# Value experts of a two-layer transformer kernel: the expert as inner index of the columns

## The chip, the cores and the metric

The kernel runs on 1 core of one Trainium2 chip. The metric is the device time of one execution in microseconds (us). One program computes the whole network, four sequences one after the other in each layer.

## The reference, cut to what matters

The network takes 4 sequences of 1024 tokens of width 256, in float32. It has four sublayers (attention, mixture of experts, attention, feed-forward), each followed by a residual sum and a layer norm. The change is in the second one. Of it:

```python
HEADS, DIM_HEAD, EXPERTS = (8, 64, 8)
gates = jax.nn.sigmoid((x @ w_gate).reshape(b, n, HEADS, EXPERTS).transpose(0, 2, 1, 3))
sel = jnp.argmax(gates, axis=-1)
gm = jax.nn.one_hot(sel, EXPERTS, dtype=x.dtype) * gates
values = jnp.einsum('bhne,ehdk,bnd->bhnk', gm, value_experts, x)
...
out = jnp.einsum('bhij,bhjk->bhik', attn, values)
out = jnp.einsum('bhne,ehkd,bhnk->bhnd', gm, output_experts, out)
```

For each head and each token the kernel computes the value of all 8 experts (8 times 64 columns), multiplies each by the gate of that expert (zero for all but one), and adds the 8 products up to 64 values.

## The kernel before, in words

Each of the four layers is a loop over four batches (sequences). A batch of layer 2 has three stages, each a block in which every engine runs its own instruction list, tied to the others by semaphores. A stage begins when all engines have finished the one before. The stages are: gates and values (`gates_and_values`, where the change is), attention, output experts.

In gates and values the input is transposed on TensorE (PE), and split into a high part `xhi` and a low part `xlo` by VectorE (DVE). VectorE then works out the gates `gm` (lines 539 to 550), and from then on goes through 64 units. A unit is one head h and one tile t of 128 tokens, heads outside, tiles inside, so a head is 8 units. For each unit n:

- TensorE makes the 128x512 product of 128 tokens with the 512 value columns of the head, in 6 matmuls (line 510), into PSUM bank n mod 7 (`RING = 7`). It waits for `value_masked` before it overwrites a bank, and at the first unit of each head for `ve_lo`.
- VectorE multiplies the 512 columns by the 8 gates into one of 6 buffers `vm` (line 559, "the mask" below).
- In two of three units VectorE itself adds the 8 experts up into 64 columns of `vx` (line 564, "the reduce"). In the third (n mod 3 = 2, `pooled(n)`) GpSimd (POOL) does so in three halving additions (lines 586 to 588, "the triple").

ScalarE (ACT) and GpSimd split the weights of each head into `vhi` (line 520, `expert_hi`) and `vlo` (line 574, `expert_lo`). The split of head h+1 stands in GpSimd's list at unit 8h+1, behind the triples of all pooled units before it. So `vlo` of head 2, which TensorE needs at unit 16, stands behind the triple of unit 8. The core of it:

```python
for n, (h, t) in enumerate(order):
    if t == 1 and 1 <= h < H0 - 1:
        expert_lo(h + 1)
    if pooled(n):
        pool.wait_ge(s.value_masked, n + 1)
```

The 512 columns of a head are laid out as 8 experts of 64 columns each: the 8 places that belong to one sum lie 64 floats (256 bytes) apart.

The next stage begins with the projections (line 635) on TensorE, which ScalarE (lines 715, 718) and VectorE (lines 749, 753) convert before the first matmul of line 648.

Of the kernel before, what the change touches and what calls it, by code (L numbers as in the profile page):

```python
# [22 lines left out]
ALU = mybir.AluOpType  # L23
# [4 lines left out]
AX_X = mybir.AxisListType.X  # L28

P = 128  # L30
# [10 lines left out]
H0, DH0, NE = 8, 64, 8  # L41
# [28 lines left out]
def bank(ps, n, lo=0, hi=HALF, rows=slice(0, P)):  # L70

    return ps[rows, n * HALF + lo:n * HALF + hi]
# [356 lines left out]
def layer2(nc, ctx, m, I, src, dst):  # L429
# [5 lines left out]
    vx = sb("vx", [P, NT, H0, P])  # L435
    oT = sb("oT", [P, H0 // 2, T])
    N = NT * H0 * NE
    gm = sb("gm", [P, N])
# [3 lines left out]
    ve, oe = sb("ve", [P, 2, KC, HALF]), sb("oe", [P, NE, D])  # L442
    half = lambda odd: slice(DH0 * odd, DH0 * odd + DH0)
    vcol = lambda h: half(h % 2)
# [25 lines left out]
    def gates_and_values(own):  # L470
        sb = lambda name, shape, dt=F32: own.enter_context(nc.sbuf_tensor("l2a_" + name, shape, dt))
        z, e, g, first = sb("z", [P, N]), sb("e", [P, N]), sb("g", [P, N]), sb("first", [P, N])
        top, win = sb("top", [P, NT * H0]), sb("win", [P, NT * H0])
        xhi, xlo = sb("xhi", [P, KC, T], F32R), sb("xlo", [P, KC, T], F32R)

        vhi, vlo = sb("vhi", [P, 2, KC, HALF], F32R), sb("vlo", [P, 2, KC, HALF], F32R)
        VM = 6
        vm = sb("vm", [P, VM, HALF])
        RING = 7
        order = [(h, t) for h in range(H0) for t in range(NT)]  # L480
        pooled = lambda n: n % 3 == 2
        pools_to = lambda n: (n + 1) // 3
        dves_to = lambda n: n + 1 - pools_to(n)
        s = s1
        with nc.Block() as block:
            @block.sync
            def _(sp):
                for h in range(2, H0):
                    sp.wait_ge(s.ve_lo, h - 1)
                    sp.dma_start(ve[:, h % 2, :, :], I["ve2"][:, :, h]).then_inc((s.even_ve_in, s.odd_ve_in)[h % 2], 16)  # L490

            @block.tensor
            def _(pe):
                entry_transpose(pe, m, s)
                for t in range(NT):
                    pe.wait_ge(s.xT_ready, t + 1)
                    for c in range(KC):
                        last = pe.matmul(bank(m.ps, 7, t * 64, t * 64 + 64), xT[:, c, t * P:(t + 1) * P], wg[:, c, :],
                                         start=(c == 0), stop=(c == KC - 1))
                last.then_inc(s.logits, 1)  # L500
                for n, (h, t) in enumerate(order):
                    if h == 0:
                        pe.wait_ge(s.x_parts, t + 1)
                    if t == 0:
                        pe.wait_ge(s.ve_lo, h + 1)
                    if n >= RING:
                        pe.wait_ge(s.value_masked, n - RING + 1)
                    for c in range(KC):
                        for x, v in ((xhi, vhi), (xhi, vlo), (xlo, vhi)):
                            last = pe.matmul(bank(m.ps, n % RING), x[:, c, t * P:(t + 1) * P], v[:, h % 2, c, :],  # L510
                                             start=(c == 0 and x is xhi and v is vhi), stop=(c == KC - 1 and x is xlo))
                    last.then_inc(s.value_mm, 1)

            @block.scalar
            def _(act):
                def expert_hi(h):
                    if h >= 2:
                        act.wait_ge((s.even_ve_in, s.odd_ve_in)[h % 2], 16 * (h // 2))
                        act.wait_ge(s.value_mm, NT * (h - 1))
                    act.copy(vhi[:, h % 2, :, :], ve[:, h % 2, :, :]).then_inc(s.ve_hi, 1)  # L520

                expert_hi(0)
                entry_copy(act, m, s, xT)
                act.wait_ge(s.exp_in, 1)
                act.activation(e[:, :], z[:, :], ACT.Exp).then_inc(s.exp_out, 1)
                for h in range(1, H0):
                    expert_hi(h)

            @block.vector
            def _(dve):  # L530
                step = Chain(dve, s.chain)
                for t in range(NT):
                    cols = slice(t * P, (t + 1) * P)
                    dve.wait_ge(s.xT_ready, t + 1)
                    dve.tensor_copy(xhi[:, :, cols], xT[:, :, cols]).then_inc(s.x_hi, 1)
                    dve.wait_ge(s.x_hi, t + 1)
                    dve.tensor_tensor(xlo[:, :, cols], xT[:, :, cols], xhi[:, :, cols].bitcast(F32), ALU.subtract).then_inc(s.x_parts, 1)
                dve.wait_ge(s.logits, 1)
                dve.tensor_scalar(z[:, :], bank(m.ps, 7), -1.0, CLAMP, ALU.mult, ALU.min).then_inc(s.exp_in, 1)
                dve.wait_ge(s.exp_out, 1)  # L540

                step(dve.tensor_scalar(z[:, :], e[:, :], 1.0, None, ALU.add))
                step(dve.reciprocal(g[:, :], z[:, :]))
                step(dve.tensor_reduce(top[:, :], by_head(g), AX_X, ALU.max))
                step(dve.tensor_tensor(by_head(first), by_head(g), every(top), ALU.is_equal))
                step(dve.tensor_tensor(by_head(first), by_head(first),
                                       prio[:, :].unsqueeze(1).to_broadcast([P, NT * H0, NE]), ALU.mult))
                step(dve.tensor_reduce(win[:, :], by_head(first), AX_X, ALU.max))
                step(dve.tensor_tensor(by_head(first), by_head(first), every(win), ALU.is_equal))
                dve.tensor_tensor(gm[:, :], first[:, :], g[:, :], ALU.mult).then_inc(s.gm_ready, 1)  # L550
                dve.wait_ge(s.gm_ready, 1)

                for n, (h, t) in enumerate(order):
                    dve.wait_ge(s.value_mm, n + 1)
                    if n >= VM:
                        k = n - VM
                        dve.wait_ge(s.pool_v_ready if pooled(k) else s.v_ready, pools_to(k) if pooled(k) else dves_to(k))
                    at = (t * H0 + h) * NE
                    dve.tensor_tensor(vm[:, n % VM, :].rearrange("p (e k) -> p e k", e=NE),
                                      bank(m.ps, n % RING).rearrange("p (e k) -> p e k", e=NE),  # L560
                                      gm[:, at:at + NE].unsqueeze(2).to_broadcast([P, NE, DH0]), ALU.mult).then_inc(s.value_masked, 1)
                    if not pooled(n):
                        dve.wait_ge(s.value_masked, n + 1)
                        dve.tensor_reduce(vx[:, t, h, vcol(h)], vm[:, n % VM, :].rearrange("p (e k) -> p k e", e=NE),
                                          AX_X, ALU.add).then_inc(s.v_ready, 1)

            @block.gpsimd
            def _(pool):
                clear(pool, s3)
                step = Chain(pool, s.pool_chain)  # L570

                def expert_lo(h):
                    pool.wait_ge(s.ve_hi, h + 1)
                    pool.tensor_tensor(vlo[:, h % 2, :, :], ve[:, h % 2, :, :], vhi[:, h % 2, :, :].bitcast(F32),
                                       ALU.subtract).then_inc(s.ve_lo, 1)

                expert_lo(0)
                entry_residual(pool, m, s)
                expert_lo(1)
                for n, (h, t) in enumerate(order):  # L580
                    if t == 1 and 1 <= h < H0 - 1:
                        expert_lo(h + 1)
                    if pooled(n):
                        pool.wait_ge(s.value_masked, n + 1)
                        slot = vm[:, n % VM, :]
                        step(pool.tensor_tensor(slot[:, 0:256], slot[:, 0:256], slot[:, 256:512], ALU.add))
                        step(pool.tensor_tensor(slot[:, 0:128], slot[:, 0:128], slot[:, 128:256], ALU.add))
                        pool.tensor_tensor(vx[:, t, h, vcol(h)], slot[:, 0:64], slot[:, 64:128], ALU.add).then_inc(s.pool_v_ready, 1)

    def attention(own, b):  # L590
        sb = lambda name, shape, dt=F32: own.enter_context(nc.sbuf_tensor("l2b_" + name, shape, dt))
# [1238 lines left out]
def layout2(i):  # L1830
    pick = np.zeros((P, H0 // 2, NE, 2), np.float32)
    for c in range(H0 // 2):
        for e in range(NE):
            for a in range(2):
                pick[(2 * c + a) * NE + e::H0 * NE, c, e, a] = 1.0
    ve = i["L0_ffn_value_experts"].transpose(2, 1, 0, 3)
    oe = i["L0_ffn_output_experts"].reshape(NE, H0 // 2, P, D).transpose(2, 1, 0, 3)
    return {
        "wq2": lay(i["L0_ffn_w_q"]), "wk2": lay(i["L0_ffn_w_k"]), "wg2": lay(i["L0_ffn_w_gate"]),
# [59 lines left out]
```

## Time and profile before

| | |
|---|---|
| median of 3 runs | 3823.37 us (3819.16 to 3826.95) |
| profiled execution | 3819.95 us, its span 3818.2 us |
| TensorE (PE) busy | 3343.3 us, 88% |
| VectorE (DVE) busy | 2084.4 us, 55% |
| ScalarE (ACT) busy | 1465.2 us, 38% |
| GpSimd (POOL) busy | 830.3 us, 22% |
| mean granted TensorE clock | 0.930 of full |
| value stage, batch 1 | first matmul of line 510 at 354.35 us, next stage's first matmul at 450.68 us |

The span is that of the instructions on the core; the execution's own time is 1.75 us longer. The shares are averages over stages with different limits, so the stage around the change has to be read by itself.

### The profile page before, as it was taken

To read this page: it belongs to the slowest core of one execution; us is meant where nothing else is said; L and a number is where in the kernel's file an instruction comes from. 1 tells how busy PE (TensorE), PEld (TensorE's weight loads), DVE (VectorE), ACT (ScalarE), POOL (GpSimd) and SP (SyncE) were. 2 spreads that over 40 slices of the span, in tenths; PEclk is the share of its full clock that TensorE was granted. 3 is DMA by queue.
4 is the path that set the end of the run, shared out by engine and by line. 5 is a ranking of instruction groups with operands and counts; after the bars stand their busy time and mean duration, and the time that the engine had idled before them with its cause. 6 is when DMAs were issued, how large, how long until landed. Compare 5 with 4: busy or idle time off the path is not lost. (4 is left out here: it accounts for less than half of the span.)

```text
span 3818.2 us, 51310 instructions
## 1 busy us (share of the span) xinstructions
PE 3343.3 (88%) x18610; PEld 2417.7 (63%) x18610; DVE 2084.4 (55%) x3495; ACT 1465.2 (38%) x2638; POOL 830.3 (22%) x908
## 2 busy tenths in 40 slices
PE   6896898988989989888998698998989698989898
PEld 4555655975568755786558555546465476767676
DVE  4346844677445954569446474756657433333333
ACT  2321144412444134431344355563645433434343
POOL 1111411743137422454216300101010000000000
PEclk9897999988999999989999899998998899999999
DMA  5111100110011100111002101000000310000000
GB/s 180 44 44 56 44 1 24 52 40 28 1 45 42 35 22 1 68 32 44 1 1 75 56 2 24 1 13 13 2 23 2 117 52 12 12 12 12 12 12 12
DMA packets 139735, 121.01 MB, mean 32 GB/s; under 512 B 79696, under 2 KB 121936, under 8 KB 136016
## 3 DMA queue, kind: packets, MB, share of 16 engines
q1 hardware_dynamic: 139472, 117.45, 10.1%
q8 instruction: 172, 2.82, 0.3%
q14 instruction: 91, 0.75, 0.1%
HBM read 100.23 MB, written 28.31 MB: 34 GB/s over the span
## 5 line engine op out<-in xcount | busy, mean ns | idle before, releaser
L1378 ACT ACTIVATE l3b_prob<-sums 128x512 f32<-128x512 f32 (+3 forms) x768 | 333.0, 494 | 205.1 <-PE sums L1311 166.6
L1628 PE MATMUL sums<-l4a_uhi,l_h 128*128 128x512 f32 x1024 | 405.8, 396 | 0.0
L1628 PE MATMUL sums<-l4a_ulo,l_h 128*128 128x512 f32 x1024 | 403.8, 394 | 0.0
L842 POOL TENSOR_TENSOR l2c_rlo<-l2c_routed,l2c_rhi 128x512 fp32r<-128x512 f32 x256 | 348.4, 1374 | 214.0 <-ACT l2c_rhi L868 177.9
L769 DVE TENSOR_REDUCE l2b_mx<-sums 128x1 f32<-128x1024 f32 (+7 forms) x256 | 192.0, 757 | 318.9 <-PE sums L650 318.2
L703 ACT ACTIVATE l2b_prob<-sums 128x512 f32<-128x512 f32 (+3 forms) x384 | 186.6, 491 | 397.7 <-PE sums L666 393.2
L1673 DVE TENSOR_TENSOR l4a_ulo<-l4a_made,l4a_uhi 128x512 fp32r<-128x512 f32 x192 | 132.1, 688 | 375.1 <-ACT l4a_uhi L1641 374.2
L222 POOL COPY sb_x<-sb_nx 128x2048 f32<-128x2048 f32 x12 | 23.0, 1914 | 1322.6 <-POOLq L1742 571.1
L952 PE MATMUL sums<-l2c_ohi,l2c_rhi 128*128 128x256 f32 x1024 | 294.4, 287 | 12.8 <-POOL l2c_rlo L842 12.1
L674 PE MATMUL sums<-l2b_prob,l_vx 128*128 128x512 f32 (+3 forms) x768 | 301.0, 506 | 3.3 <-ACT l2b_den L725 1.9
L1306 PE MATMUL sums<-l_qst,l_kst 64*128 64x512 f32 (+3 forms) x768 | 279.3, 427 | 16.4 <-DMA l_qst<-l3b_peak 6.7
L952 PE MATMUL sums<-l2c_ohi,l2c_rlo 128*128 128x256 f32 x1024 | 291.9, 285 | 0.0
L952 PE MATMUL sums<-l2c_olo,l2c_rhi 128*128 128x256 f32 x1024 | 291.8, 285 | 0.0
L785 POOL TENSOR_SCALAR l2b_shift<-sb_ident,l2b_mx 128x128 fp32r<-128x128 f32 x256 | 154.2, 605 | 603.7 <-DVE l2b_mx L769 491.0
L1289 PE MATMUL sums<-l_kst,l_qst 64*128 64x512 f32 (+3 forms) x768 | 244.1, 443 | 18.9 <-DVE l3b_low L1390 10.4
L905 DVE TENSOR_TENSOR l2c_routed<-l_oT,sums 128x512 f32<-128x512 f32 x256 | 171.6, 682 | 149.3 <-PE sums L942 148.2
L868 ACT CAST l2c_rhi<-l2c_routed 128x512 fp32r<-128x512 f32 x256 | 158.2, 621 | 238.2 <-DVE l2c_routed L905 236.8
L1306 PEld LDWEIGHTS sums<-l_qst,l_kst 64*128 64x128 f32 x768 | 140.8, 195 | 153.9 <-ACT l3b_prob L1378 133.6
L203 PE MATMUL sums<-sb_ident,sb_nx 128*128 128x128 f32 x256 | 61.0, 421 | 194.4 <-issue 93.0
L1628 PEld LDWEIGHTS sums<-l4a_uhi,l_h 128*128 128x128 f32 x1024 | 192.4, 188 | 47.5
L1628 PEld LDWEIGHTS sums<-l4a_ulo,l_h 128*128 128x128 f32 x1024 | 192.4, 188 | 45.6
L662 PE MATMUL sums<-l2b_qst,l2b_kst 128*128 128x512 f32 (+3 forms) x384 | 207.5, 540 | 7.9 <-POOL l2b_shift L785 7.9
(247 smaller groups left out, 8141.3 us busy)
## 6 DMA issues: line engine op xcount, KB each, us to landing
l_ve<-ve SPq DMA_DIRECT2D x34, 512.0 KB, 4.0
l_oe<-oe SPq DMA_DIRECT2D x16, 1024.0 KB, 6.2
sb_nx<-sums SPq DMA_DIRECT2D x15, 1024.0 KB, 5.5
l2c_word<-weights_copy SPq DMA_DIRECT2D x32, 352.0 KB, 4.0
weights_copy<-h SPq DMA_DIRECT2D x2, 4096.0 KB, 25.9
l_qst<-l3b_peak SPq DMA_DIRECT2D x512, 0.5 KB, 2.0
l_h<-weights_copy SPq DMA_DIRECT2D x2, 4096.0 KB, 23.9
sb_nx<-tokens SPq DMA_DIRECT2D x5, 1024.0 KB, 5.7
```

The costliest lines, as they stand in the source:

```text
L662: pe.matmul(out, keys, qst[:, h % RK, lo:hi], start=True, stop=False)
L674: last = pe.matmul(bank(m.ps, PV, lo, hi), vx[:, k, h, :], prob[:, k % 2, lo:hi], start=(k == 0), stop=True, skip_group_check=True)
L703: act.activation(prob[:, k % 2, lo:hi], bank(m.ps, n % 3, 0, hi - lo), ACT.Exp, scale=SCALE0).then_inc(s.exp_ready, 1)
L769: dve.reduce_max(mx[:, h1, t:t + 1], bank(m.ps, max_bank(h1, k), 0, (t + 1) * P), AX_X).then_inc(s.max_read, 1)
L842: pool.tensor_tensor(rlo[:, i % RT, :], routed[:, i % RT, :], rhi[:, i % RT, :].bitcast(F32), ALU.subtract).then_inc(s.routed_lo, 1)
L868: act.copy(rhi[:, i % RT, :], routed[:, i % RT, :]).then_inc(s.routed_hi, 1)
L905: dve.tensor_tensor(routed[:, i % RT, :], oT[:, c, n * HALF:(n + 1) * HALF], bank(m.ps, 4 + i % 4), ALU.mult).then_inc(s.routed, 1)
L952: last = pe.matmul(m.ps[:, t * D:(t + 1) * D], r[:, k % RT, cols], w[:, c % 2, e, :], start=(c == e == 0 and t % 2 == 0 and r is rhi and w ...
L1289: last = pe.matmul(bank(m.ps, at, 0, hi - lo), qst[rows(a), p, t * P:(t + 1) * P], kst[rows(a), p, lo:hi], start=True, stop=True)
L1306: last = pe.matmul(bank(m.ps, part % SCORE, 0, hi - lo), kst[rows(a), p, k * P:(k + 1) * P], qst[rows(a), p, lo:hi], start=True, stop=True)
L1378: act.activation(prob[:, i % RB, j, a, 0:hi - lo], bank(m.ps, part % SCORE, 0, hi - lo), ACT.Exp, scale=SCALE1).then_inc(s.exp_ready, 1)
L1628: run(lambda out, a, x, first, last: pe.matmul(out, a, x, start=first, stop=last))
```

## The change

The columns of the value weights are laid out with the expert as inner index (on the host, in `layout2`), so that the 8 places of a sum are neighbours. The mask, the reduce and the triple follow with their access patterns. The mask now repeats the 8 gates 64 times, where it repeated each gate 64 times. The triple adds runs of 4, then of 2 places, at a pitch of 8 places, and last two single places. Numbers of instructions, sizes, waits, buffers and DMAs stay as they are.

```diff
+        by_key = lambda x: x.rearrange("p (k e) -> p k e", e=NE)
...
-                    dve.tensor_tensor(vm[:, n % VM, :].rearrange("p (e k) -> p e k", e=NE),
-                                      bank(m.ps, n % RING).rearrange("p (e k) -> p e k", e=NE),
-                                      gm[:, at:at + NE].unsqueeze(2).to_broadcast([P, NE, DH0]), ALU.mult).then_inc(s.value_masked, 1)
+                    dve.tensor_tensor(by_key(vm[:, n % VM, :]), by_key(bank(m.ps, n % RING)),
+                                      gm[:, at:at + NE].unsqueeze(1).to_broadcast([P, DH0, NE]), ALU.mult).then_inc(s.value_masked, 1)
                     if not pooled(n):
                         dve.wait_ge(s.value_masked, n + 1)
-                        dve.tensor_reduce(vx[:, t, h, vcol(h)], vm[:, n % VM, :].rearrange("p (e k) -> p k e", e=NE),
-                                          AX_X, ALU.add).then_inc(s.v_ready, 1)
+                        dve.tensor_reduce(vx[:, t, h, vcol(h)], by_key(vm[:, n % VM, :]), AX_X, ALU.add).then_inc(s.v_ready, 1)
...
-                        slot = vm[:, n % VM, :]
-                        step(pool.tensor_tensor(slot[:, 0:256], slot[:, 0:256], slot[:, 256:512], ALU.add))
-                        step(pool.tensor_tensor(slot[:, 0:128], slot[:, 0:128], slot[:, 128:256], ALU.add))
-                        pool.tensor_tensor(vx[:, t, h, vcol(h)], slot[:, 0:64], slot[:, 64:128], ALU.add).then_inc(s.pool_v_ready, 1)
+                        slot = by_key(vm[:, n % VM, :])
+                        step(pool.tensor_tensor(slot[:, :, 0:4], slot[:, :, 0:4], slot[:, :, 4:8], ALU.add))
+                        step(pool.tensor_tensor(slot[:, :, 0:2], slot[:, :, 0:2], slot[:, :, 2:4], ALU.add))
+                        pool.tensor_tensor(vx[:, t, h, vcol(h)], slot[:, :, 0], slot[:, :, 1], ALU.add).then_inc(s.pool_v_ready, 1)
...
-    ve = i["L0_ffn_value_experts"].transpose(2, 1, 0, 3)
+    ve = i["L0_ffn_value_experts"].transpose(2, 1, 3, 0)
```

## Rows read from the trace of the kernel before

**Rows 1.** Busy time by engine, batch 1's value stage from unit 16 on

```profile
core 0: us, PE busy (x) PEld busy (x) DVE busy (x) ACT busy (x) POOL busy (x), PEclk, DMA share, GB/s
...
380.50:446.20 65.70, 65.57 (x288) 53.98 (x288) 64.56 (x82) 4.22 (x4) 37.40 (x56) 1.00 0.10 33
```

**Rows 2.** Groups by form on VectorE: shapes xcount | busy us, mean ns | idle before

```profile
L564 DVE TENSOR_REDUCE l_vx<-l2a_vm 128x64 f32<-128x512 f32 x172 | 184.5, 1073 | 5.9
...
L559 DVE TENSOR_TENSOR l2a_vm<-sums,l_gm 128x512 f32<-128x512 f32 x256 | 167.2, 680 | 0.1
L1390 DVE TENSOR_REDUCE l3b_low<-sums 128x2 f32<-128x1024 f32 x128 | 156.4, 1222 | 24.2 <-PE sums L1289 24.1
...
L1196 DVE TENSOR_REDUCE l3a_drift<-l3a_h 128x8 f32<-128x1024 f32 x4 | 4.9, 1220 | 0.1
...
L546 DVE TENSOR_TENSOR l2a_first<-l2a_first,l_prio 128x512 f32<-128x512 f32 x4 | 2.8, 691 | 0.1
...
L548 DVE TENSOR_REDUCE l2a_win<-l2a_first 128x64 f32<-128x512 f32 x4 | 2.7, 686 | 0.1
```

**Rows 3.** Groups by form on GpSimd, same columns

```profile
L574 POOL TENSOR_TENSOR l2a_vlo<-l_ve,l2a_vhi 128x1024 fp32r<-128x1024 f32 x32 | 76.6, 2393 | 113.1 <-ACT l2a_vhi L520 113.1
L586 POOL TENSOR_TENSOR l2a_vm<-l2a_vm 128x256 f32<-128x256 f32 x84 | 61.9, 737 | 166.2 <-DVE l2a_vm L559 166.2
...
L587 POOL TENSOR_TENSOR l2a_vm<-l2a_vm 128x128 f32<-128x128 f32 x84 | 38.8, 462 | 6.6
L588 POOL TENSOR_TENSOR l_vx<-l2a_vm 128x64 f32<-128x64 f32 x84 | 27.1, 322 | 6.6
```

**Rows 4.** Timeline of batch 1 around unit 8's mask and unit 16's matmuls

```profile
start us, us, engine line op out<-in xcount [idle before <-releaser]
375.74 1.28 DVE L559 TENSOR_TENSOR l2a_vm<-sums,l_gm 128x512 f32<-128x512 f32 x2
...
376.50 0.73 POOL L586 TENSOR_TENSOR l2a_vm<-l2a_vm 128x256 f32<-128x256 f32 x1 [2.32 <-DVE l2a_vm L559]
...
378.13 2.36 POOL L574 TENSOR_TENSOR l2a_vlo<-l_ve,l2a_vhi 128x1024 fp32r<-128x1024 f32 x1
...
380.55 0.50 PE L510 MATMUL sums<-l2a_vhi,l2a_xhi 128*128 128x512 f32 x1 [2.06 <-POOL l2a_vlo L574]
```

**Rows 5.** The same timeline of batches 2, 3 and 4, at unit 16

```profile
830.15 0.50 PE L510 MATMUL sums<-l2a_vhi,l2a_xhi 128*128 128x512 f32 x1 [2.22 <-POOL l2a_vlo L574]
...
1280.43 0.80 PE L510 MATMUL sums<-l2a_vhi,l2a_xhi 128*128 128x512 f32 x1 [2.27 <-POOL l2a_vlo L574]
...
1283.16 0.63 PE L510 MATMUL sums<-l2a_vhi,l2a_xhi 128*128 128x512 f32 x1
...
1728.19 0.50 PE L510 MATMUL sums<-l2a_vhi,l2a_xhi 128*128 128x512 f32 x1 [1.78 <-POOL l2a_vlo L574]
```

**Rows 6.** Timeline of the end of batch 1's value stage

```profile
445.73 0.39 PE L510 MATMUL sums<-l2a_vhi,l2a_xlo 128*128 128x512 f32 x1
...
449.23 1.02 DVE L564 TENSOR_REDUCE l_vx<-l2a_vm 128x64 f32<-128x512 f32 x1
...
450.01 0.32 POOL L588 TENSOR_TENSOR l_vx<-l2a_vm 128x64 f32<-128x64 f32 x1
```

**Rows 7.** TensorE's timeline of the next stage's start, all four batches

```profile
450.68 5.37 PE L635 MATMUL sums<-l_xT,l_wk 128*128 128x512 f32 x8 [4.56 <-PEq L485]
...
465.86 1.22 PE L648 MATMUL sums<-l2b_kst,l2b_qst 128*128 128x512 f32 x2 [6.38 <-DVE l2b_qlo L753]
...
900.30 5.98 PE L635 MATMUL sums<-l_xT,l_wk 128*128 128x512 f32 x8 [4.57 <-PEq L485]
...
916.10 1.22 PE L648 MATMUL sums<-l2b_kst,l2b_qst 128*128 128x512 f32 x2 [6.38 <-DVE l2b_qlo L753]
...
1350.54 3.67 PE L635 MATMUL sums<-l_xT,l_wk 128*128 128x512 f32 x8 [2.97 <-PEq L485]
...
1364.03 1.22 PE L648 MATMUL sums<-l2b_kst,l2b_qst 128*128 128x512 f32 x2 [6.39 <-DVE l2b_qlo L753]
...
1798.34 5.82 PE L635 MATMUL sums<-l_xT,l_wk 128*128 128x512 f32 x8 [4.53 <-PEq L485]
...
1813.97 1.22 PE L648 MATMUL sums<-l2b_kst,l2b_qst 128*128 128x512 f32 x2 [6.38 <-DVE l2b_qlo L753]
```

## The prediction

> **What bounds the kernel now.** The chain of work that ended last lies wholly in the last layer, so it says nothing of this change. I therefore took the value stage by itself, first with the busy time of its window, then with the groups of its instructions, then with the timeline at the places where TensorE stood still.
>
> The window shows two engines that are both nearly full. From unit 16 to the end of the stage TensorE is busy for 65.57 of 65.70 us and VectorE for 64.56 [rows 1]. The paces are close: 288 matmuls in 65.7 us are 0.228 us each, 1.37 us a unit of six, 4.11 us for three units. VectorE's three units are three masks and two reduces, 3 x 0.680 + 2 x 1.073 = 4.19 us by the mean durations [rows 2]. In the timeline neighbours overlap slightly. The triples show the true period: GpSimd's start at 376.50 came after 0.08 us behind the mask, and each such start is 4.0 us after the one before (1.63 us for a triple up to the next instruction at 378.13, and 2.32 us of idle time ahead [rows 4]). So VectorE goes at 4.0 us and TensorE at 4.1 us for three units. TensorE sets the pace in the long run. VectorE starts late, because it works out the gates first while TensorE fills the banks, and catches up hardly at all. The reader should see that a cheaper reduce cannot buy 172 times its saving: TensorE's 87 us of matmuls in the stage stay. It buys what VectorE's lateness costs TensorE, and that is at two places.
>
> The first is unit 16. GpSimd's low part of head 2's weights stands behind the triple of unit 8, which waits for VectorE's mask. It starts at 378.13 and takes 2.36 us, and TensorE has stood still for 2.06 us when it resumes at 380.55 [rows 4]. The other batches lose 2.22, 2.27 and 1.78 us there [rows 5].
>
> The second is the end. TensorE's last matmul starts at 445.73 and ends at 446.12, VectorE's last reduce ends at 449.23 + 1.02 = 450.25, and GpSimd's last addition at 450.33 [rows 6]. The next stage's first matmul starts at 450.68. TensorE's gap is 4.56, 4.57, 2.97 and 4.53 us in the four batches [rows 7].
>
> **The change, part by part.**
>
> *The reduce* (43 a batch, 172 in all). It reads 8 neighbours instead of 8 places 256 bytes apart. Line 548 does the new form already: 128x64 from 128x512, neighbours, in 686 ns against 1073 [rows 2]. It is a maximum and not a sum, but over 1024 elements the sum of line 1196 takes 1220 ns and line 1390's reduction, which is no sum, 1222, so the operation does not set the price. I take 686, a saving of 0.387 us each; the bounds are 0 (the stride is not what costs) and 0.387.
>
> *The mask* (256). PSUM and the output are read and written in the same order as before. Only the gates' pattern turns: 8 places repeated, as `prio` is in line 546, at 691 ns with both inputs in SBUF, against 680 for the mask now [rows 2]. I take no change; the upper bound of 11 ns is 0.1 us in the nine masks ahead of unit 16 and is hidden elsewhere.
>
> *The triple* (84). 256, 128 and 64 elements take 737, 462 and 322 ns [rows 3], so (462 - 322)/64 = 2.2 ns an element and about 180 ns to start. No GpSimd row of this trace reads with a stride, so the price x added to a triple is unknown. Below, x is 0: the runs of 4 and 2 places are neighbours. It cannot be a gain, since contiguous is the best form these rows show. Above, the nearest row is VectorE's reduce, 1073/686 = 1.56 times [rows 2]; on all 1.52 us of a triple that is x = 0.85 us. Only the third addition steps over 8 places for each element; the same 56% on it alone is 0.18 us. I take x = 0.2, since the first two additions still read runs.
>
> The Trainium skill has a rule that speaks against this part: the GPSIMD Engine Reference, section "Performance pitfalls for Q7 kernels", says that a GpSimd read with an inner step above 8 bytes costs about 50% more per element. Only the third addition has such a step (32 bytes), and 50% on its 64 x 2.2 ns would be an estimate of 0.07 us, so by that rule the sum below would be 0.2 us larger. No row here can show whether the runs of 4 and 2 escape the rule.
>
> *The sum.* I call a TensorE wait "gone" where the late engine is earlier than TensorE by then.
>
> 1. Unit 16. Ahead of unit 8's mask VectorE has done six reduces (units 0, 1, 3, 4, 6, 7), so the mask comes 6 x 0.387 = 2.32 us earlier, and the triple and the low part behind it 2.32 - 0.2 = 2.12. The waits of 2.06 and 1.78 go, those of 2.22 and 2.27 shrink to 0.10 and 0.15: 8.33 - 0.25 = 8.1 us.
> 2. Clock behind that wait. In batch 3 alone the wait is followed by matmuls at half clock: from 1280.43 to 1283.16 are 6 starts [rows 5] in 2.73 us, where 6 x 0.228 = 1.37. With a wait of 0.15 I expect full clock: 1.4 us.
> 3. The end. VectorE gains (4.1 - 3.23)/3 = 0.29 us a unit on TensorE (3.23 = 4.0 - 2 x 0.387). It begins about eight units' time behind (unit 0's mask comes at 364, its matmuls were done by 357), so it has caught up after some 30 units and then waits for TensorE. After the last matmul come a wait (0.05, my allowance), mask 0.68, 0.04, reduce 0.69 and the 0.43 us between VectorE's end and the next matmul (450.68 - 450.25 [rows 6, 7]): a gap of 1.9 us in each batch. GpSimd's way, the triple of unit 62, is shorter: it starts one unit (1.37) earlier, and -1.37 + 0.05 + 0.68 + 0.08 + 1.65 + 0.35 + x = 1.44 + x, so x up to 0.45 is hidden there. The gaps now are 16.63 us in sum; 16.6 - 7.6 = 9.0 us.
> 4. Clock behind the end. From the first projection to the first matmul of line 648 the batches take 15.18, 15.80, 13.49 and 15.63 us. The short one is batch 3, whose gap was 2.97 us: its first 8 matmuls took 3.67 us against 5.37 to 5.98 [rows 7]. The granted clock fell toward its lower level of 1.2 GHz in the gaps of 4.5 us, and did not in that of 2.97. With gaps of 1.9 I expect 13.5 in all: 1.7 + 2.3 + 2.1 = 6.1 us.
>
> In all 8.1 + 1.4 + 9.0 + 6.1 = 24.6 us. Everything behind it (attention, output experts, the loads that SP issues at the stage's start) moves forward with it: the next batch's input and the first output experts are loaded behind the whole attention stage. The ring of 7 banks is not a new bound: VectorE frees a bank in 3.23/3 = 1.08 us, TensorE wants one in 1.37. GpSimd has time: in 24 units (32.9 us) it does eight triples of 1.65 and three low parts of 2.39 [rows 3], 20.4 us. The other low parts come about eight units ahead of their need, which covers x until GpSimd is full.
>
> Against the profiled execution's 3819.95 us this gives 3795.4. The median of the runs is 3.4 us above that execution, so I predict 3799 for the median.
>
> **Rivals.**
>
> *The clock does not follow.* Terms 2 and 4 stay away, because it falls at moments that the gaps alone do not explain: 2.22 us at unit 16 left it full and 2.27 did not [rows 5]. For it speaks just that; against it batch 3's start at full clock [rows 7]. Gain 17.1: 3806.
>
> *The triple gets dearer by about 1 us* (a cost for each short run). Then the waits at unit 16 stay at 0.74, 0.90, 0.95 and 0.46 (the triple and low part come 2.32 - 1 earlier), 3.1 us in sum against 0.25, and the end is set by GpSimd, 1 - 0.45 = 0.55 later, 2.2 us. The gain is 24.6 - 2.8 - 2.2 = 19.6: 3804.
>
> *GpSimd becomes the bound* (the other side). It has 21 triples and six low parts (2 to 7), 6 x 2.39 = 14.3 us, from its first mask at about 367.7 on. It ends as late as now, at 450.3, with triples of (450.3 - 367.7 - 14.3)/21 = 3.25 us, twice the 1.65 of now. Beyond that each 0.1 us costs 21 x 4 x 0.1 = 8.4 us. If it priced its 64 rows of 4 and of 2 singly and the triple took 4 us, it would add 63 us: 3886. For it speaks that no row shows such a pattern; against it the bound of 1.56 times from VectorE's row [rows 2].
>
> *The reduce does not get cheaper.* If the 1073 ns came from summing rather than stride, nothing moves: 3823. Rows of line 1196 and 1390 speak against it [rows 2].
>
> **How the numbers follow.** The forecast has 0.57, the clock rival 0.20, the dearer triple 0.11, GpSimd as the bound 0.06, no gain 0.04; 0.02 is left for the unseen. A measurement of this kernel tells 0.2%, 7.6 us, from no change. Faster takes the first three, 0.89; the same 0.05; slower 0.06. The forecast alone spans 3793 to 3805: x from 0 to 0.85 costs up to 4 us, and the runs scatter by 4 us either way. The range reaches over the clock rival and the dearer triple, with a little for clock falls elsewhere: 3789 to 3813.
>
> **What the profile after would show.** Line 564 at about 686 ns, line 559 at 680 to 691. No wait of line 510 for line 574 above 0.3 us. VectorE idle in the second half of the stage, waiting for line 510, which it never does now. Gaps ahead of line 635 of about 1.9 us in all batches and 13.5 us from there to line 648. Lines 586 to 588 at 737, 462 and 322 ns plus at most 0.2 us in sum. The prediction is wrong if line 588 or the two before it double, if line 564 stays above 0.8 us, or if other stages' clock falls move.

## The result and the profile after

The changed kernel takes 3798.13 us (median of 5 runs, 3789.5 to 3801.19) against 3823.37 us before (now 5 runs, 3819.1 to 3835.22), a ratio of 0.9928 with a 95% interval of 0.9905 to 0.995. That is 25 us faster, where 24.6 were forecast; the interval itself reaches from 19 to 36 us. The profiled execution took 3800.84 us, its span is 3799.1.

The groups of instructions by form, which answer to [rows 2, 3]; the lines have moved by one:

```profile
L560 DVE TENSOR_TENSOR l2a_vm<-sums,l_gm 128x512 f32<-128x512 f32 x256 | 173.8, 688 | 37.2 <-PE sums L511 37.0
L564 DVE TENSOR_REDUCE l_vx<-l2a_vm 128x64 f32<-128x512 f32 x172 | 118.0, 686 | 5.9
...
L585 POOL TENSOR_TENSOR l2a_vm<-l2a_vm 128x256 f32<-128x256 f32 x84 | 61.2, 729 | 150.9 <-DVE l2a_vm L560 149.7
L586 POOL TENSOR_TENSOR l2a_vm<-l2a_vm 128x128 f32<-128x128 f32 x84 | 33.7, 401 | 6.6
L587 POOL TENSOR_TENSOR l_vx<-l2a_vm 128x64 f32<-128x64 f32 x84 | 25.8, 308 | 6.6
```

The reduce went from 1073 to 686 ns. The mask now waits 37.0 us for TensorE, where it waited 0.1 us before: VectorE has changed from the engine that is waited for to the one that waits. GpSimd's triple became cheaper, 1.44 us instead of 1.52, although its accesses now step over places.

Where each engine stood shows in the busy time of batch 1's value stage, from the first mask to the last reduce. First the kernel before:

```profile
core 0: us, PE busy (x) PEld busy (x) DVE busy (x) ACT busy (x) POOL busy (x), PEclk, DMA share, GB/s
364.30:450.30 86.00, 79.76 (x351) 65.41 (x349) 84.45 (x107) 6.32 (x6) 45.98 (x69) 1.00 0.08 25
```

and then the changed one:

```profile
363.60:443.20 79.60, 79.55 (x351) 65.52 (x349) 68.87 (x106) 6.32 (x6) 43.44 (x67) 1.00 0.08 27
```

Before, VectorE is busy for 84.45 of 86.00 us (the rest is the few hundredths between its instructions) and TensorE for 79.76. After, TensorE is busy for 79.55 of 79.60 us. The stretch is now as long as TensorE's work in it.

At the places that [rows 5, 7] show, TensorE's timeline of the changed kernel has:

```profile
444.93 3.67 PE L634 MATMUL sums<-l_xT,l_wk 128*128 128x512 f32 x8 [1.77 <-PEq L486]
...
458.41 1.22 PE L647 MATMUL sums<-l2b_kst,l2b_qst 128*128 128x512 f32 x2 [6.38 <-DVE l2b_qlo L752]
...
888.29 3.67 PE L634 MATMUL sums<-l_xT,l_wk 128*128 128x512 f32 x8 [1.78 <-PEq L486]
...
901.77 1.22 PE L647 MATMUL sums<-l2b_kst,l2b_qst 128*128 128x512 f32 x2 [6.38 <-DVE l2b_qlo L752]
...
1263.99 0.50 PE L511 MATMUL sums<-l2a_vhi,l2a_xhi 128*128 128x512 f32 x1 [0.52 <-POOL l2a_vlo L573]
...
1706.85 0.50 PE L511 MATMUL sums<-l2a_vhi,l2a_xhi 128*128 128x512 f32 x1 [0.39 <-POOL l2a_vlo L573]
```

The gaps are 1.77 or 1.78 us in all four batches, and from the first projection to line 647 all four take 13.48 us. The wait at unit 16 is gone in batches 1 and 2 and 0.52 and 0.39 us in batches 3 and 4.

Since runs of one kernel scatter by 10 to 20 us, I compare the experiments by a local length too, read from the profiled execution of each: from the value stage's table load on ScalarE (343.23 us in batch 1 before) to the first matmul of line 648, which begins the attention's maxima (465.86; line 647 in the changed kernel), summed over the four batches. I call it the stage sum. It is 490.38 us before and 463.67 after.

### The profile page after: what moved, and what is told of

Read it like the earlier page. It is cut to its first block and busy times, and to the rows that moved or that the text cites. A ratio compares the mean times of both kernels' runs of the same rounds, so it can differ in the third digit from the quotient of the medians.

```text
span 3799.1 us, 51310 instructions
## 1 busy us (share of the span) xinstructions
PE 3341.0 (88%) x18610; PEld 2420.0 (64%) x18610; DVE 2027.6 (53%) x3495; ACT 1465.0 (39%) x2638; POOL 822.0 (22%) x908
## 5 line engine op out<-in xcount | busy, mean ns | idle before, releaser
L1305 PE MATMUL sums<-l_qst,l_kst 64*128 64x512 f32 (+3 forms) x768 | 278.5, 428 | 16.6 <-DMA l_qst<-l3b_peak 7.4
```

The lines of the kernel that those rows point to most:

```text
L1305: last = pe.matmul(bank(m.ps, part % SCORE, 0, hi - lo), kst[rows(a), p, k * P:(k + 1) * P], qst[rows(a), p, lo:hi], start=True, stop=True)
```

## The experiments

**The reduce alone.**

```diff
-dve.tensor_reduce(vx[...], vm[:, n % VM, :].rearrange("p (e k) -> p k e", e=NE),
+dve.tensor_reduce(vx[...], vm[:, n % VM, :].rearrange("p (k e) -> p k e", e=NE),
```

> The kernel before with only the reduce's access pattern changed to 8 neighbouring places; weights, mask and triple stay as before, so the values are sums over the wrong places. Theory 1 (VectorE's lateness): the reduce takes 686 ns and the whole gain of the change is here, 25 us, time about 3798; the gap ahead of the projections is 1.8 us in each batch. Theory 2 (the faster triple has a part in it): some microseconds are missing, 3800 to 3806. On GpSimd: if the 462 ns of the second addition fell to 400 because VectorE's strided reduce no longer disturbs it, it reads 400 here too; if its own new pattern did it, it stays at 462.

It took 3799.28 us, ratio 0.9941 (0.9926 to 0.9956); the stage sum is 464.42. The whole gain is there with the reduce alone. On GpSimd the old pattern has its old price:

```profile
L587 POOL TENSOR_TENSOR l2a_vm<-l2a_vm 128x128 f32<-128x128 f32 x84 | 38.7, 461 | 6.6
```

So it is the triple's own pattern that makes it cheaper, not a calmer VectorE beside it.

**The triple alone.**

```diff
-slot = vm[:, n % VM, :]
-step(pool.tensor_tensor(slot[:, 0:256], slot[:, 0:256], slot[:, 256:512], ALU.add))
...
+slot = vm[:, n % VM, :].rearrange("p (k e) -> p k e", e=NE)
+step(pool.tensor_tensor(slot[:, :, 0:4], slot[:, :, 0:4], slot[:, :, 4:8], ALU.add))
...
```

> The kernel before with only GpSimd's triple changed to runs of 4, 2 and 1 place; weights, mask and reduce stay as before, so a third of the values are sums over the wrong places. Theory 1: VectorE is as late as before, nothing moves by more than 0.1 us a batch, 3823 within noise; waits at unit 16 about 2.0 us. Theory 2: up to 5 us faster. On GpSimd: 400 ns for the second addition if its own pattern is cheaper, 462 if VectorE's strided reduce is what slows it.

3820.68 us, ratio 0.9995 (0.9984 to 1.0005), stage sum 491.54: no gain. The second addition took 404 ns, beside the strided reduce too.

**The wait at unit 16 alone, in the kernel before.**

```diff
-if t == 1 and 1 <= h < H0 - 1:
+if n == NT - 2:
+    expert_lo(2)
+if t == 1 and 2 <= h < H0 - 1:
     expert_lo(h + 1)
```

> The kernel before, with the low part of head 2 ahead of the triple of unit 8 in GpSimd's list, so that TensorE's wait at unit 16 goes and nothing else changes. Theory 1: VectorE works without a pause from the gates to the stage's end, so TensorE comes 2 us earlier and then waits 2 us longer at the end; the gap grows from 4.5 to 6.6 us, the time stays at 3823 within 2 us. Rival (each wait of TensorE costs by itself, the waits at unit 16 are worth their 8.3 us alone): 3815 or, with the clock of batch 3, 3813.

3825.61 us, ratio 1.0011 (1.0 to 1.0022), stage sum 493.08. No gain; if anything a loss, 2.7 us by the stage sum. The wait went away and came back elsewhere. TensorE's timeline of batch 1:

```profile
400.51 0.50 PE L510 MATMUL sums<-l2a_vhi,l2a_xhi 128*128 128x512 f32 x1 [0.61 <-POOL l2a_vlo L574]
...
412.55 0.50 PE L510 MATMUL sums<-l2a_vhi,l2a_xhi 128*128 128x512 f32 x1 [0.87 <-POOL l2a_vlo L574]
...
450.47 6.02 PE L637 MATMUL sums<-l_xT,l_wk 128*128 128x512 f32 x8 [4.99 <-PEq L485]
```

TensorE now waits at later heads, because GpSimd's list is still tied to the late masks, and 4.99 us at the end; 0.61 + 0.87 + (4.99 - 4.56) = 1.91 of the 2.06 us are accounted for. The gap did not reach 6.6 us, because I had overlooked the later low parts. The stage's end did not move, as VectorE's gapless list sets it: I had named two places that cost time, and they are two signs of one lateness. The plainest sign is the length from the first mask to the next stage's first matmul: 86.4 us in each of the four batches before (450.68 - 364.31 in batch 1), 86.4 with this edit, and 81.2 to 81.6 in the changed kernel. The 2.7 us are nearly all batch 3's: its gap grew from 2.97 to 5.03 us, and the way from the projections to line 648's matmul from 13.49 to 15.78.

**The same in the changed kernel**, the same diff.

> The changed kernel with the same edit. Theory 1: TensorE now sets the end, so the 0.91 us of waits left at unit 16 in two batches are gained in full, 1 us in all, below what a measurement can tell: 3797. Rival (GpSimd's order still matters more): 3 us or more.

3797.24 us, ratio 0.9937 (0.9922 to 0.9952), stage sum 462.55, 1.1 us less than the change's. With TensorE setting the end, that wait counts in full; it is too small for the clock on the wall.

**VectorE's lateness given back, in the changed kernel.**

```diff
 dve.tensor_reduce(vx[:, t, h, vcol(h)], by_key(vm[:, n % VM, :]), AX_X, ALU.add).then_inc(s.v_ready, 1)
+spare = (top, win)[dves_to(n) % 2]
+dve.tensor_reduce(spare[:, 0:33], z[:, 0:264].rearrange("p (k e) -> p k e", e=NE), AX_X, ALU.add)
```

> The changed kernel with a second small reduce of 264 elements into a spare tile behind each reduce, about 0.39 us from start to start, which gives VectorE back what the change took away; the layout, mask and triple stay new. Theory 1 (lateness): the time is that of the kernel before, 3820 to 3826, with waits at unit 16 of about 2 us and gaps of 3 to 4.5 us. Rival (the layout gains otherwise: triple, memory traffic): it keeps part of the gain, 3805 to 3815.

3815.32 us, ratio 0.9975 (0.9961 to 0.9989), stage sum 481.18. That is at the upper edge of the rival's range and not in mine. The timeline shows why: 365.65 - 364.71 = 0.94 us from a reduce to the next mask, where the kernel before has 0.98 (365.04 to 366.02), 43 times a batch.

```profile
364.71 0.69 DVE L564 TENSOR_REDUCE l_vx<-l2a_vm 128x64 f32<-128x512 f32 x1
365.31 0.42 DVE L566 TENSOR_REDUCE l2a_win<-l2a_z 128x33 f32<-128x264 f32 x1
365.65 0.68 DVE L560 TENSOR_TENSOR l2a_vm<-sums,l_gm 128x512 f32<-128x512 f32 x1
```

To see whether that is all of it, I made the padding longer.

> The changed kernel with padding reduces of 288 instead of 264 elements: the first padding made VectorE 0.36 us slower a reduce from start to start and left its stage end 1.3 us a batch ahead of the kernel before; 24 elements more should add 0.025 us each, 1.1 us a batch. Theory 1: the stage from the table load to line 647 takes 488 to 492 us in four batches (490.38 before, 463.67 after), the time is 3820 to 3824. Rival: it stays 5 us or more below the kernel before.

With 288 elements 3814.08 us, ratio 0.9977 (0.9966 to 0.9989), stage sum 483.44: again short, and by more than the rival's 5 us. I had reckoned the shortfall from the stage's end with 264 elements, but TensorE set that end in three of the four batches (gaps of 2.10 us) and so hid a part of it. The step itself, now 0.96 us, is the measure.

> The changed kernel with padding reduces of 312 elements. From the start of one reduce to the next mask were 0.98 us before, 0.94 with 264 and 0.96 with 288 elements, so 312 give 0.98. Theory 1: VectorE needs 85.9 us from the first mask to the last reduce's end as before, the gaps are about 4.5 us again, the stage to line 647 takes 489 to 493 us in four batches and the time is that of the kernel before, 3819 to 3826. Rival (the new layout or triple gains by itself, or the padding is not equal to the old reduce for another reason): 3 us or more below it.

With 312 elements 3820.6 us, ratio 0.999 (0.9976 to 1.0004), stage sum 490.14 against 490.38 before. The median is 3.0 us below that of the kernel before in the same series, just where the rival began, but the interval includes no change, and the stage sum, which is finer, differs by 0.24 us. From the first mask, 363.84, to the end of the last padding, 449.25 + 0.47, are 85.9 us, as before (364.31 to 450.25):

```profile
363.84 0.69 DVE L560 TENSOR_TENSOR l2a_vm<-sums,l_gm 128x512 f32<-128x512 f32 x1
364.57 0.69 DVE L564 TENSOR_REDUCE l_vx<-l2a_vm 128x64 f32<-128x512 f32 x1
365.17 0.47 DVE L566 TENSOR_REDUCE l2a_win<-l2a_z 128x39 f32<-128x312 f32 x1
365.56 0.68 DVE L560 TENSOR_TENSOR l2a_vm<-sums,l_gm 128x512 f32<-128x512 f32 x1
...
449.25 0.47 DVE L566 TENSOR_REDUCE l2a_win<-l2a_z 128x39 f32<-128x312 f32 x1
```

Within these limits the new layout with the old VectorE time is the old kernel. The three steps from a reduce to the next mask, 0.94, 0.96 and 0.99 us, give stage sums of 481.2, 483.4 and 490.1: a few hundredths 43 times over decide which engine sets the end.

**Another relief of VectorE, without the change.** Every second unit is added up on GpSimd in place of every third.

```diff
-pooled = lambda n: n % 3 == 2
-pools_to = lambda n: (n + 1) // 3
+pooled = lambda n: n % 2 == 0
+pools_to = lambda n: n // 2 + 1
```

> The kernel before in its old layout, with every second unit (n even) added up on GpSimd instead of every third, so that VectorE has 32 instead of 43 of the 1073 ns reduces a batch. Theory 1 (the gain is VectorE's lateness, however it is relieved): unit 16's wait falls to 0.1 us, VectorE catches up, the gaps are 2.2 us (the last reduce is still the long one), and the time is 3800, within 3 us of the changed kernel, with no change of layout. Rival (the layout itself gains, or GpSimd with 32 triples becomes the bound): above 3810.

3798.82 us, ratio 0.9941 (0.9926 to 0.9955), stage sum 468.88, in the old layout and with the reduce at 1077 ns. VectorE's mask now waits for TensorE there:

```profile
L559 DVE TENSOR_TENSOR l2a_vm<-sums,l_gm 128x512 f32<-128x512 f32 x256 | 171.2, 684 | 24.6 <-PE sums L510 24.3
```

Most of the gain needs neither the layout nor a cheap reduce, only that VectorE is no longer late. By the stage sum it is 21.5 of the 26.7 us. Of the 5.2 us that are missing, 1.3 are longer gaps (2.1 us each) and 1.7 a lower clock behind one of them; the runs as a whole can't tell the two kernels apart.

> The changed kernel with the same edit. Theory 1: VectorE already waits for TensorE, so a further relief of VectorE buys nothing beyond the rest of the wait at unit 16 (1 us in all): 3796 to 3799, gaps of 1.8 us. Rival (VectorE is still a bound): 3790 or less.

The same on top of the change: 3795.65 us, ratio 0.9939 (0.9922 to 0.9955), stage sum 464.10 against 463.67. Nothing is added.

**The gap and the clock.** Extra work on VectorE after the last unit makes only the gap ahead of the projections longer.

```diff
+for i in range(4):    # 2 in the other kernel
+    step(dve.tensor_tensor(z[:, :], first[:, :], g[:, :], ALU.mult))
```

> The changed kernel with four extra 128x512 multiplications on VectorE after the last unit of the value stage, 4 x 0.72 = 2.9 us, so that only the gap ahead of the projections is made as long as before, 4.66 us. If the clock follows the gap: first projection to line 647 takes 15.2 to 15.8 us instead of 13.48, and the time is 4 x 2.9 + 4 x 2 = 19.6 us above the changed kernel, about 3818. If the clock has another cause: 13.48 us stays, 11.5 us above, 3810.

3819.49 us, ratio 0.999 (0.9979 to 1.0), stage sum 487.84. That is 21 us above the changed kernel, 24 by the stage sum, for 4 x 3.0 = 12 us of longer gaps. From the first projection to the maxima it takes 16.41, 16.46, 15.74 and 14.89 us, 9.6 more in sum than 4 x 13.48. The 9.6 us are clock: with the same instructions, only the pause ahead of them differs. The other 2.6 us of the stage sum lie between the first mask and the last matmul, 2.4 of them in batches 2 and 3. There TensorE had come to unit 7 early, stood still for 4.36 and 3.69 us until the first mask freed a bank, and went on at half clock; the granted clock from first mask to last matmul is 0.96 and 0.98, against 1.00 in batch 1. This is read from the trace and was not tested by itself.

```profile
446.93 6.59 PE L636 MATMUL sums<-l_xT,l_wk 128*128 128x512 f32 x8 [4.76 <-PEq L486]
...
811.99 0.77 PE L511 MATMUL sums<-l2a_vhi,l2a_xhi 128*128 128x512 f32 x1 [4.36 <-DVE l2a_vm L560]
```

> The same with two extra multiplications: gaps of 3.2 us, near the 2.97 us of batch 3 before. If the clock falls only in longer gaps: 13.48 us to line 647 in all batches and 5.8 us above the changed kernel, 3804. If it falls in proportion to the gap: 14 to 15 us, 3807 to 3809.

3803.71 us, ratio 0.995 (0.9934 to 0.9966), stage sum 473.53. The time is the first theory's, by luck, for neither had the mechanism right: of four gaps of 3.3 us two were followed by full clock and two were not.

```profile
446.87 5.37 PE L636 MATMUL sums<-l_xT,l_wk 128*128 128x512 f32 x8 [3.32 <-PEq L486]
...
893.02 3.67 PE L636 MATMUL sums<-l_xT,l_wk 128*128 128x512 f32 x8 [3.35 <-PEq L486]
```

**Single instructions.** Blocks behind the last layer, on spare tiles.

```diff
+def reduce(dve, pitch):
+    dve.tensor_reduce(y[:, :].rearrange("p (a b) -> p a b", b=pitch),
+                      x[:, :].rearrange("p (a e b) -> p a b e", e=NE, b=pitch), AX_X, ALU.add)
...
+for pitch in (1, 2, 4, 8, 16, 64):
+    for _ in range(3):
+        reduce(dve, pitch)
```

> The changed kernel with separate blocks behind the last layer that measure single instructions on spare tiles: VectorE sums of 8 places into 64 with a pitch of 1, 2, 4, 8, 16 and 64 floats, and GpSimd's three additions in the old and the new form, each with VectorE idle, doing reduces of pitch 64, and doing reduces of pitch 1. Expected on VectorE: 686 ns at pitch 1 and 1073 at 64; by the page SBUF of the Trainium skill, which puts the limit of free strides at 16 bytes, the step would lie between pitch 2 and pitch 4 or 8; a gradual rise would speak for a cost in proportion to the bytes stepped over. Expected on GpSimd: if the form sets the time, 737, 462 and 322 ns in the old form beside any partner; if VectorE's strided reads set it, about 400 for the second addition in both forms beside pitch 1 or an idle VectorE, and 462 only beside pitch 64.

The probes ran once, for their durations alone. VectorE's reduces in windows of this sequence, with shortest, median and longest time in ns; the windows' edges fall inside the groups of three:

```profile
L1806 DVE TENSOR_REDUCE probe_y<-probe_x x3: 686/686/686, 3814.2 to 3815.6; 128x64 f32<-128x512 f32 x3
...
L1806 DVE TENSOR_REDUCE probe_y<-probe_x x3: 687/1056/1057, 3816.4 to 3818.2; 128x64 f32<-128x512 f32 x3
...
L1806 DVE TENSOR_REDUCE probe_y<-probe_x x3: 1058/1066/1066, 3819.3 to 3821.5; 128x64 f32<-128x512 f32 x3
...
L1806 DVE TENSOR_REDUCE probe_y<-probe_x x3: 1011/1012/1012, 3826.8 to 3828.9; 128x64 f32<-128x512 f32 x3
```

The first six reduces (pitch 1 and 2, the sixth at 3816.4) take 686 ns, those with pitch 4 1057, with 8 1066, with 16 1005, and with 64 1012. It is one step, between 8 and 16 bytes, not a slope. (Why the kernel's own reduce took 1073 ns at 64 was not looked into.) GpSimd, the old form beside reduces of pitch 1, then the new form beside reduces of pitch 64 (the first number is the 128-element addition, the last the 256-element one):

```profile
L1822 POOL TENSOR_TENSOR probe_u<-probe_u x6: 452/588/724, 3842.8 to 3847.0; 128x256 f32<-128x256 f32 x3, 128x128 f32<-128x128 f32 x3
...
L1822 POOL TENSOR_TENSOR probe_u<-probe_u x6: 398/563/726, 3855.1 to 3859.2; 128x256 f32<-128x256 f32 x3, 128x128 f32<-128x128 f32 x3
```

The form sets the time beside all three partners (VectorE idle, pitch 64, pitch 1): 724 to 726, 452 to 453 and 317 to 319 ns in the old one, 724 to 727, 398 and 297 to 303 in the new.

## Why the prediction was right, point by point

*What bounds the stage.* Right: VectorE's lateness, and TensorE behind it, at 79.6 us for the same stretch. My wording of it, two places where it costs, was not: the experiment that removes the wait at unit 16 by itself gained nothing. Before the change VectorE's 85.9 us from first mask to last reduce are the path. The terms of my sum are TensorE's side of the ledger, and they add up only if all go at once.

*The reduce*, 0.387 us: measured exactly so, and alone it gives the whole gain. *The mask*: 688 against 680 ns, within the bound, hidden.

*The triple*: a step that failed. I took x = 0.2 us and wrote that it "cannot be a gain". It was one, -0.08 us, since contiguous is not the best form there. The rule that the Trainium skill gives for kernels written for GpSimd's own cores (GPSIMD Engine Reference, section "Performance pitfalls for Q7 kernels", about 50% more per element for an inner step above 8 bytes) does not show in this ready-made addition: the third one, with a step of 32 bytes, went from 322 to 308 ns. Neither mattered, as this triple is off the path.

*Term 1 and 2*, the wait at unit 16 and the half clock behind it, 9.5 us. TensorE's matmuls of the stage, first to last start, took 367.1 us in four batches before and 356.6 after (89.15, 89.38, 89.02 and 89.06), so 10.5. The way from unit 0 to unit 16 was set by VectorE through GpSimd: 380.55 - 354.35 = 26.2 us before [rows 4], and 1263.99 - 1240.16 = 23.8 after in batch 3, which is VectorE's lead of 2.32 us and the triple's 0.08. I had counted TensorE's waits instead, which are smaller. The waits left are 0.91 us, with 0.25 foretold, and both are above the 0.3 us that I had named as the most. They are in the two batches in which TensorE's clock rose early (4 and 6 half-clock matmuls at the stage's start, against 10 and 11 in the others), so that it came to unit 16 sooner; this is read from the trace and was not tested by itself. The half-clock matmuls behind unit 16 in batch 3 are gone, as forecast.

*Term 3*, the gaps, 9.0 us: from 16.63 to 7.11, so 9.5. I had 1.9 us for a gap that is 1.78. VectorE waited for TensorE for the first time at unit 24 (390.15 us in batch 1), where I had said 30; my own numbers, 364 - 357 = 7 us made up at 0.29 us a unit, give 24.

*Term 4*, the clock behind the gap, 6.1 us: from 60.10 to 53.92, 6.2. The mechanism holds (the four extra multiplications brought a loss of 9.6 us), but it was less sure than I made it from one batch. For gaps between 2.1 and 3.6 us the rival, by which the clock does not follow the gap, was partly right. The gaps of 1.78 us lie below all of these.

In sum 26.2 us, and 0.55 at the stage's start make the 26.7 of the stage sum. That the medians differ by 25.2 us, so near the forecast 24.6, is in part luck. The profiled execution gained only 3819.95 - 3800.84 = 19.1 (I had said 3795.4 for it). The first batch's variance line of layer 3 (line 1110 before, 1109 after) starts 25.5 us earlier (2175.1 and 2149.6), so 6.4 us were lost later, in layers that the change does not touch. Of these, 5.3 lie in one stretch of layer 4, between the same two matmuls of line 1628 (1627 after). First before, then after, with the columns of [rows 1]:

```profile
3283.90:3763.40 479.50, 435.46 (x2001) 355.89 (x2000) 175.60 (x391) 184.69 (x285) 3.79 (x2) 0.96 0.03 11
3259.30:3744.10 484.80, 440.48 (x2002) 358.85 (x2001) 175.99 (x391) 184.56 (x285) 3.79 (x2) 0.95 0.03 11
```

The work and the transfers are the same, and the granted clock is 0.95 where it was 0.96, which over 480 us is 5 us. So one of my signs of being wrong did appear: clock falls in another stage moved. It is no fixed price of the change: four of the ten traces with the new reduce, that of the reduce alone among them, have 479.6 to 480.0 us in this stretch. But the other six have 481.9 to 486.5, and the four with the old reduce 479.5 to 480.0, so whether the change makes such falls more frequent is open.

## What to carry to other kernels

When two engines run a stage at nearly one pace, read both from the first common unit to the last: the one that is busy without a gap is the path, and waits of the other are its shadow. A saving on it is worth its sum only until the other takes over: here 43 x 0.387 = 16.6 us a batch bought 26.7/4 = 6.7, and a further relief bought nothing. Look also at what a shorter pause does to the next stage's clock. And before a layout is changed for a late engine, try moving units to an idle one: two edited lines gave the same time within the scatter of the runs, and four fifths of the gain by the stage sum.

## What was not expected of the hardware

- A sum of 8 places into 64 on VectorE takes 686 ns with its places 4 or 8 bytes apart and 1005 to 1066 from 16 bytes on (1073 in the kernel), and 256 bytes are hardly worse than 16. The Trainium skill's page SBUF — State Buffer (section "Door 1: The DMA port swizzle") says that full bandwidth needs at least two hits in a line of 16 bytes, and gives 4 fp32 as how far one can stride for free. The trace agrees with the first: a pitch of 2 floats costs nothing. Against the second, a pitch of 4 floats already costs the full step (1057 ns).
- GpSimd adds 128 elements in 398 to 404 ns when they lie in runs of 2 at a pitch of 8, and in 452 to 462 ns when they are contiguous, whatever VectorE does beside it.
- TensorE's clock behind a pause. The projections after a gap of 1.8 us ran at full clock (their first 8 matmuls in 3.67 us) in 16 of 16 batches (the change, the reduce alone, the early low part and the half pooled one on top of it). Of 19 gaps of 2.1 to 3.6 us, in seven kernels, 8 were followed by a stretch below it (5.3 to 6.4 us). After gaps of 4.4 us and more it was 17 of 17. Between 2.1 and 3.6 us the length of the pause alone did not decide.
